# Field-pair projection on one Trainium2 core: the loop over batch tiles is replaced, on all five engines, by sixteen tiles written out

## The chip, the cores and the metric

The kernel runs on one core of one Trainium2 chip. The metric is the device time of one execution in microseconds; less is better. The core has a TensorE (PE) for matrix products, a VectorE (DVE), a ScalarE (ACT), a GpSimd (POOL), and a SyncE (SP) that here only issues transfers. Each engine has its own stream of instructions, and they meet only at semaphores. The transfers of the core are carried out by 16 DMA engines.

## The reference, cut to what matters

```python
# x: (2048, 32, 64) f32, W: (496, 64, 64) f32, PAIRS: all (i, j) with i < j < 32
xi = x[:, pi, :]
xj = x[:, pj, :]
proj = jnp.einsum('bpd,pod->bpo', xi, W)
return proj * xj                      # (2048, 496, 64) f32
```

For each of the 496 pairs of fields, field i is projected with the pair's own 64x64 matrix and multiplied element by element with field j. The input is 16.8 MB, the weights are 8.1 MB, and the output is 260 MB.

## The kernel before, in words

The batch of 2048 rows is cut into 16 tiles of 128 rows (`tiles`, line 74). All weights stay in SBUF (`w_sb`, line 134): even fields in partitions 0 to 63, odd fields in 64 to 127, so that a step works on two fields, one for each half of the rows of the PE array. A tile has 21 steps (`plan`, line 25; a step is a pair of lists of segments, one for each half), and the steps are bundled into 11 output groups. One group leaves by one DMA (line 183), whose 128 rows of 7 to 15 KB are spread over the DMA engines.

The stages of a step, each on its own engine, linked by semaphores:

- PE (`project`, line 275; matmul at line 284) writes two halves of a PSUM buffer `proj[b][h]`. The two buffers b are used in turn.
- DVE (line 326) multiplies the first half with `x_sb` and writes it to `staged`. The second half of two steps in three (`pool_steps`, line 93) is copied out by ACT (line 250) and then multiplied in place by POOL (line 213); of the other steps DVE does both halves.
- SP (lines 170 to 184) waits until a group is complete and issues its store.

`staged` has nine slots for the eleven groups of a tile: groups 9 and 10 share slots 4 and 5 with the groups of those numbers (`SHARED_SLOTS`, line 17). Before a slot is written again its last store must have landed (`slot_free`, line 156; waited for by DVE and ACT). Between steps 9 and 10 PE transposes the next tile's `x` ("turn", line 291), ACT copies it into `x_t` (line 228), and before step 3 ACT issues the load of the x tile after that (`load_x`, line 231).

Every engine's stream is an `emit(tile)` that yields one tile's instructions, and `each_tile` (line 119) strings the tiles together: tile 0 written out, then a counted loop of seven rounds over two tiles (tiles 1 to 14), then tile 15 written out. Inside the loop a tile's number is a register expression, so that the values that semaphores are waited for (`use + 1`, `tile.number + 1`, `tile.number * 16 * ...`) and the DRAM addresses of the stores and x loads (lines 183 and 237) are computed by small register instructions before the instruction that uses them. The first and the last tile have constants there. The loop is each engine's own: there is no barrier between the engines at its end.

Of the kernel before, what the change touches and what calls it, by code (L numbers as in the profile page):

```python
# [71 lines left out]
def field_pair_project(nc, x, w, ident, out, fields, dim):  # L72
    batch = x.shape[0]
    tiles = batch // P
# [40 lines left out]
    def w_needed(segments):  # L115
        to = max(w_at[i] + (j - i - 1 + n) * dim for i, j, n in segments)
        return next(c for c in range(len(w_cuts) - 1) if w_cuts[c + 1] >= to)

    def each_tile(eng, emit):
        emit(Tile(0, 0, 0))  # L120
        with eng.Fori(0, (tiles - 2) // 2) as t:  # L121
            emit(Tile(2 * t + 1, 1, t))
            emit(Tile(2 * t + 2, 0, t + 1))
        emit(Tile(tiles - 1, 1, tiles // 2 - 1, last=True))

    with ExitStack() as ctx:  # L126
# [41 lines left out]
        @block.sync  # L168
        def _(sp):
            def emit(tile):  # L170
                where = {item: (b, use) for item, b, use in items(tile)}
                for g, group in enumerate(groups):
                    first, n = group_range(g)


                    pooled = any(s in pool_steps for s in group)
                    if pooled and g == 0:
                        sp.wait_ge(pool_scaled[g], tile.number + 1)
                    b, use = where[group[-1]]
                    sp.wait_ge(emptied[b][group[-1] not in pool_steps], use + 1)  # L180
                    if pooled and g > 0:
                        sp.wait_ge(pool_scaled[g], tile.number + 1)  # L182
                    sp.dma_start(out[bass.ds(tile.number * P, P), first * dim:(first + n) * dim],  # L183
                                 staged[slot_of[g]][:, 0:n * dim]).then_inc(stored[slot_of[g]], 16)

            half = fields * dim // 2
            sp.dma_start(x_sb[0][:, 0:half], x[0:P, 0:half]).then_inc(x_first_loaded[0], 16)
            sp.dma_start(w_sb[:, w_cuts[0]:w_cuts[1]], w[:, w_cuts[0]:w_cuts[1]]).then_inc(w_loaded[0], 16)
            sp.dma_start(x_sb[0][:, half:], x[0:P, half:]).then_inc(x_first_loaded[1], 16)
            for c in range(1, len(w_cuts) - 2):  # L190
                sp.dma_start(w_sb[:, w_cuts[c]:w_cuts[c + 1]], w[:, w_cuts[c]:w_cuts[c + 1]]
                             ).then_inc(w_loaded[c], 16)

            c = len(w_cuts) - 2
            sp.dma_start(w_sb[0:dim, w_cuts[c]:w_cuts[c + 1]], w[0:dim, w_cuts[c]:w_cuts[c + 1]]
                         ).then_inc(w_loaded[c], 16)
            sp.dma_start(x_sb[1][:], x[P:2 * P, :]).then_inc(x_loaded[1], 16)

            each_tile(sp, emit)
            for k in range(slots):  # L200
                sp.wait_ge(stored[k], 16 * slot_uses[k] * tiles)

        @block.gpsimd
        def _(pool):
            def emit(tile):
                for item, b, use in items(tile):
                    if item not in pool_steps:
                        continue
                    for i, j, n in steps[item][1]:
                        product = staged_part(item, i, j, n)  # L210

                        pool.wait_ge(emptied[b][1], use + 1)  # L212
                        last = nc.gpsimd.tensor_tensor(  # L213
                            product, product, x_sb[tile.parity][:, j * dim:(j + n) * dim], ALU.mult)
                    g = group_of[item]
                    if item == max(s for s in groups[g] if s in pool_steps):
                        last.then_inc(pool_scaled[g], 1)

            each_tile(pool, emit)

        @block.scalar
        def _(act):
            act.dma_start(ident_sb[:], ident).then_inc(ident_loaded, 16)

            def turned_out(b, use, to):
                for h in range(2):
                    act.wait_ge(filled[b][h], use + 1)
                    nc.scalar.activation(x_t[to][:, h * (UNIT // P):(h + 1) * (UNIT // P), :].rearrange(  # L228
                        "p k b -> p (k b)"), proj[b][h][:], ACT.Copy).then_inc(emptied[b][h], 1)

            def load_x(tile):

                _, b, use = list(items(Tile(tile.number - 1, 1 - tile.parity, None)))[-1]

                act.wait_ge(emptied[b][1], use + 1)
                act.wait_ge(pool_scaled[group_of[pool_steps[-1]]], tile.number)
                act.dma_start(x_sb[1 - tile.parity][:], x[bass.ds((tile.number + 1) * P, P), :]
                              ).then_inc(x_loaded[1 - tile.parity], 16)

            def emit(tile):  # L240
                for item, b, use in items(tile):
                    if item == LOAD_BEFORE and not tile.first and not tile.last:
                        load_x(tile)
                    if item == "turn":
                        turned_out(b, use, 1 - tile.parity)
                    elif item in pool_steps:
                        (i, j, n), = steps[item][1]
                        slot_free(act, tile, group_of[item])
                        act.wait_ge(filled[b][1], use + 1)  # L249
                        nc.scalar.activation(staged_part(item, i, j, n), proj[b][1][:, 0:n * dim],  # L250
                                             ACT.Copy).then_inc(emptied[b][1], 1)

            turned_out(0, 0, 0)
            each_tile(act, emit)

        @block.tensor
        def _(pe):
            def turn(b, of, h):

                for n in range(UNIT // P):  # L260
                    k = h * (UNIT // P) + n
                    last = nc.tensor.transpose(proj[b][h][:, n * P:(n + 1) * P],  # L262
                                               x_sb[of][:, k * P:(k + 1) * P], ident_sb[:])
                last.then_inc(filled[b][h], 1)

            def pieces(segments):

                for (i, j, n), at in zip(segments, place(segments, dim)):
                    col, left = w_at[i] + (j - i - 1) * dim, n * dim
                    while left:  # L270
                        width = min(left, BANK - at % BANK)
                        yield i, col, at, width
                        at, col, left = at + width, col + width, left - width

            def project(tile, s, b, use):
                if tile.first:
                    for h in range(2):
                        pe.wait_ge(w_loaded[w_needed(steps[s][h])], 16)
                for h in range(2):
                    if not (tile.first and use == 0):  # L280
                        pe.wait_ge(emptied[b][h], use)
                    half = slice(h * dim, (h + 1) * dim)
                    for i, col, at, width in pieces(steps[s][h]):
                        last = nc.tensor.matmul(  # L284
                            proj[b][h][:, at:at + width], x_t[tile.parity][half, i // 2, :],
                            w_sb[half, col:col + width], start=True, stop=True)
                    last.then_inc(filled[b][h], 1)

            def emit(tile):
                for item, b, use in items(tile):  # L290
                    if item == "turn":
                        pe.wait_ge(x_loaded[1 - tile.parity], 16 * tile.half + 16)
                        for h in range(2):
                            pe.wait_ge(emptied[b][h], use)
                            turn(b, 1 - tile.parity, h)
                    else:
                        project(tile, item, b, use)

            pe.wait_ge(ident_loaded, 16)
            for _ in range(WARM_UP):  # L300
                nc.tensor.transpose(proj[1][0][:, 0:P], ident_sb[:], ident_sb[:])  # L301
            for h in range(2):
                pe.wait_ge(x_first_loaded[h], 16)
                turn(0, 0, h)
            for h in range(2):

                pe.wait_ge(emptied[0][h], 1)
            each_tile(pe, emit)

        @block.vector  # L310
        def _(dve):
# [16 lines left out]
                                x_sb[tile.parity][:, j * dim:(j + n) * dim], ALU.mult)  # L328
                        last.then_inc(emptied[b][h], 1)

            each_tile(dve, emit)


# [28 lines left out]
```

## Time and profile before

| | |
|---|---|
| time, median of 3 runs | 691.28 us (691.06 to 692.1) |
| profiled execution, its own time | 692.27 us |
| its span (first to last instruction) | 690.5 us |
| granted TensorE clock, mean | 0.904 |
| PE / PEld / DVE / ACT / POOL busy | 87 / 54 / 60 / 30 / 57% |
| moved by DMA | 285.15 MB, mean 413 GB/s |
| DMA queues: output and first loads (q1), x loads (q10) | 93.3% and 5.8% of 16 engines |
| instruction packets (q8, q14) | 5 of 16 KB, 5 of 8 KB |

Busy shares are of the span. The profiled execution is 1.0 us above the median of the three runs; 1.8 us of it lie around the span. A queue's share is the time of its packets, as a share of 16 engines' span; packets that overlap can bring a sum slightly over 100%. Register, branch, semaphore and DMA-issuing instructions are not counted as busy.

### The profile page before, as it was taken

The numbers are of one execution on the slowest core, as the hardware profiler recorded it, in microseconds if no ns is written. First come the engines' busy times: TensorE is split into PE (matmuls) and PEld (weight loads), VectorE is DVE, ScalarE is ACT, GpSimd is POOL, SyncE is SP. The second block draws the span as 40 slices with busy tenths as digits, with TensorE's granted clock in tenths as the row PEclk, the third lists the DMA queues.
The fourth block names the chain that finished last, engine by engine and source line by source line (L and its number), as shares of the span: only waits on it lengthen the run. The fifth ranks groups of instructions, "written<-read, shape, count | busy, mean of one in ns | idle before, by whom it ended". The sixth has DMA issues, their size and how long they took to land.

```text
span 690.5 us, 8403 instructions
## 1 busy us (share of the span) xinstructions
PE 597.8 (87%) x2704; PEld 372.9 (54%) x2704; DVE 415.0 (60%) x528; ACT 205.4 (30%) x257; POOL 390.7 (57%) x228
## 2 busy tenths in 40 slices
PE   6889979799797989979799797988979799797972
PEld 4556646466464555646466464645646466464641
DVE  0656646576574756647576474856747576474851
ACT  2322414233241332414223241322414224141320
POOL 0745738457474655738557374755738557374651
PEclk9998989899897998989989898997989989898995
DMA  8999999999999999999999999999999999999897
GB/s 332 386 430 425 431 427 429 426 428 427 423 427 429 392 417 411 427 426 407 428 407 431 406 427 428 412 425 376 424 423 405 428 415 423 414 423 427 357 422 316
DMA packets 29754, 285.15 MB, mean 413 GB/s; under 512 B 3312, under 2 KB 3440, under 8 KB 7216
## 3 DMA queue, kind: packets, MB, share of 16 engines
q1 hardware_dynamic: 27584, 270.28, 93.3%
q10 hardware_dynamic: 2160, 14.75, 5.8%
q8 instruction: 5, 0.08, 0.0%
q14 instruction: 5, 0.04, 0.0%
HBM read 24.97 MB, written 260.05 MB: 413 GB/s over the span
## 4 chain that ended last, share of the span: by engine, by line
DMA 37%; POOL 26%; issue 22%; PE 10%; ACT 2%; DVE 1%; POOLq 0%; SPq 0%; DVEq 0%; ACTq 0%
DMA out_dram<-staged 36%; POOL staged L213 26%; PE proj L284 9%; ACT staged L250 2%; DVE staged L326 1%; DMA ident_sb<-ident_dram 1%; PE proj L301 1%; POOLq L212 0%; PE proj L262 0%; ACT x_t L228 0%; SPq L183 0%; POOLq L121 0%; ACTq L249 0%; DVEq L126 0%; SPq L182 0%
## 5 line engine op out<-in xcount | busy, mean ns | idle before, releaser
L284 PE MATMUL proj<-w_sb,x_t 64*128 64x512 f32 (+7 forms) x2432 | 562.3, 564 | 72.5 <-DVE staged L326 70.1
L326 DVE TENSOR_TENSOR staged<-proj,x_sb 128x1024 f32<-128x1024 f32 (+7 forms) x528 | 415.0, 828 | 264.5 <-PE proj L284 187.0
L213 POOL TENSOR_TENSOR staged<-staged,x_sb 128x1024 f32<-128x1024 f32 (+4 forms) x224 | 390.5, 1755 | 284.6 <-ACT staged L250 283.8
L284 PEld LDWEIGHTS proj<-w_sb,x_t 64*128 64x128 f32 x2432 | 339.2, 205 | 288.5 <-issue 132.1
L250 ACT ACTIVATE staged<-proj 128x1024 f32<-128x1024 f32 (+4 forms) x224 | 172.8, 787 | 453.0 <-PE proj L284 344.6
L262 PEld LDWEIGHTS proj<-ident_sb,x_sb 128*128 128x128 f32 x256 | 30.4, 150 | 10.2 <-issue 7.6
L262 PE MATMUL proj<-ident_sb,x_sb 128*128 128x128 f32 x256 | 34.1, 290 | 1.9 <-DMA x_sb<-x_dram 1.9
L228 ACT ACTIVATE x_t<-proj 128x1024 f32<-128x1024 f32 x32 | 31.2, 1022 | 13.7 <-PE proj L262 12.2
L301 PE MATMUL proj<-ident_sb 128*128 128x128 f32 x16 | 3.7, 425 | 5.7 <-DMA ident_sb<-ident_dram 5.7
L301 PEld LDWEIGHTS proj<-ident_sb 128*128 128x128 f32 x16 | 3.3, 227 | 5.7 <-DMA ident_sb<-ident_dram 5.7
L228 ACT ACT_TABLE_LOAD x1 | 1.3, 1283 | 1.2 <-PEq L356 1.2
L356 POOL MEMSET const-float32-0.0<- 128x1 f32 x1 | 0.1, 98 | 0.2 <-issue 0.2
L356 POOL MEMSET const-bfloat16-1.0<- 128x1 bf16 x1 | 0.1, 101 | 0.0
L356 POOL MEMSET const-uint8-127<- 128x1 uint8 x1 | 0.1, 101 | 0.0
L356 POOL MEMSET const-float32-1.0<- 128x1 f32 x1 | 0.1, 98 | 0.0
## 6 DMA issues: line engine op xcount, KB each, us to landing
out_dram<-staged SPq DMA_DIRECT2D x16, 1952.0 KB, 11.4
out_dram<-staged SPq DMA_DIRECT2D x16, 1824.0 KB, 14.2
out_dram<-staged SPq DMA_DIRECT2D x16, 1728.0 KB, 17.3
out_dram<-staged SPq DMA_DIRECT2D x16, 1696.0 KB, 14.8
out_dram<-staged SPq DMA_DIRECT2D x16, 1568.0 KB, 14.3
out_dram<-staged SPq DMA_DIRECT2D x16, 1440.0 KB, 15.7
out_dram<-staged SPq DMA_DIRECT2D x16, 1312.0 KB, 15.6
out_dram<-staged SPq DMA_DIRECT2D x16, 1216.0 KB, 13.8
```

The source lines that it names most:

```text
L213: last = nc.gpsimd.tensor_tensor(product, product, x_sb[tile.parity][:, j * dim:(j + n) * dim], ALU.mult)
L228: nc.scalar.activation(x_t[to][:, h * (UNIT // P):(h + 1) * (UNIT // P), :].rearrange("p k b -> p (k b)"), proj[b][h][:], ACT.Copy).then_i ...
L250: nc.scalar.activation(staged_part(item, i, j, n), proj[b][1][:, 0:n * dim], ACT.Copy).then_inc(emptied[b][1], 1)
L262: last = nc.tensor.transpose(proj[b][h][:, n * P:(n + 1) * P], x_sb[of][:, k * P:(k + 1) * P], ident_sb[:])
L284: last = nc.tensor.matmul(proj[b][h][:, at:at + width], x_t[tile.parity][half, i // 2, :], w_sb[half, col:col + width], start=True, stop=True)
L301: nc.tensor.transpose(proj[1][0][:, 0:P], ident_sb[:], ident_sb[:])
L326: last = nc.vector.tensor_tensor(staged_part(item, i, j, n), proj[b][h][:, at:at + n * dim], x_sb[tile.parity][:, j * dim:(j + n) * dim], ...
L356: nc = bacc.Bacc("TRN2", target_bir_lowering=False, num_devices=1)
```

## The change

A second helper, `every_tile`, calls `emit` sixteen times with plain numbers: parity and half as before, `last` for tile 15. All five engines use it in place of `each_tile`. The tiles, their order, the steps, the waits and the transfers stay what they are; in tiles 1 to 14 the counts that are waited for and the DRAM addresses become constants, the register instructions and the seven backward branches of each engine are gone, and each engine's instruction stream is about four times as long (16 tiles of code in place of 4).

```diff
+    def every_tile(emit):
+
+        for t in range(tiles):
+            emit(Tile(t, t % 2, t // 2, last=t == tiles - 1))
+
...
-            each_tile(sp, emit)
+            every_tile(emit)
...
-            each_tile(pool, emit)
+            every_tile(emit)
...
             turned_out(0, 0, 0)
-            each_tile(act, emit)
+            every_tile(emit)
...
-            each_tile(pe, emit)
+            every_tile(emit)
...
-            each_tile(dve, emit)
+            every_tile(emit)
```

## Rows read from the trace of the kernel before

**Rows 1.** The page: instructions per engine, queues by kind (packets, MB, share)

```profile
PE 597.8 (87%) x2704; PEld 372.9 (54%) x2704; DVE 415.0 (60%) x528; ACT 205.4 (30%) x257; POOL 390.7 (57%) x228
...
q1 hardware_dynamic: 27584, 270.28, 93.3%
q10 hardware_dynamic: 2160, 14.75, 5.8%
q8 instruction: 5, 0.08, 0.0%
q14 instruction: 5, 0.04, 0.0%
```

**Rows 2.** Waits: engine line <- what: us, times, longest

```profile
ACT staged L250 <- DMA out_dram<-staged: 107.9, 16, 7.3
DVE staged L326 <- DMA out_dram<-staged: 73.7, 16, 5.2
PE proj L284 <- DVE staged L326: 70.1, 16, 5.0
...
PE proj L284 <- issue: 1.2, 1, 1.2
```

**Rows 3.** Stretches: PE, PEld, DVE, ACT, POOL busy; PEclk, DMA share, GB/s

```profile
135.00:640.00 505.00, 450.02 (x2037) 279.56 (x2039) 314.66 (x403) 154.13 (x194) 295.70 (x170) 0.91 1.00 419
...
475.00:485.00 10.00, 10.00 (x47) 5.95 (x45) 8.08 (x8) 3.78 (x4) 6.60 (x4) 0.97 0.82 333
645.10:647.30 2.20, 2.20 (x9) 1.15 (x8) 2.20 (x3) 0.81 (x1) 2.20 (x2) 1.00 0.05 22
686.40:689.20 2.80, 0.00 (x0) 0.00 (x0) 0.00 (x0) 0.00 (x0) 0.00 (x0) 0.50 0.07 30
```

**Rows 4.** The chain that ended last: two pieces of one tile (start, us)

```profile
384.08 0.71 ACT staged L250
...
409.44 16.02 DMA out_dram<-staged
```

**Rows 5.** Instruction packets in 0:135, in 135:640 (all its queues), in 640:690.5

```profile
q8 instruction: 4, 0.07, 0.2%
q14 instruction: 4, 0.03, 0.1%
...
q1 hardware_dynamic: 19410, 198.79, 93.4%
q10 hardware_dynamic: 1728, 12.58, 6.8%
...
q8 instruction: 1, 0.02, 0.2%
q14 instruction: 1, 0.01, 0.0%
```

**Rows 6.** One q8 packet in 29:31, 86:88, 647:649; one q14 packet in 76:77

```profile
q8 instruction: 1, 0.02, 3.4%
q8 instruction: 1, 0.02, 2.8%
q8 instruction: 1, 0.02, 4.1%
...
q14 instruction: 1, 0.01, 1.9%
```

**Rows 7.** DMA in 647.38:647.46: packets by queue

```profile
q8 instruction: 1, 0.02, 101.4%
q1 hardware_dynamic: 1, 0.01, 29.4%
```

**Rows 8.** Line 121, the loop's end: ns min/median/max

```profile
L121 PEldq FUSED_REGOPS  x7: 59/59/59, 53.0 to 551.5; - x7
...
L121 PEldq ALU_OP  x7: 32/32/32, 136.0 to 634.2; - x7
L121 PEldq COMPARE_BRANCH  x7: 76/208/228, 136.1 to 634.3; - x7
```

**Rows 9.** Register work of PE (L281), POOL (L212) and SP (L183) in the loop

```profile
L281 PEldq ALU_OP  x154: 32/32/42, 54.8 to 628.4; - x154
...
L212 POOLq ALU_OP  x140: 32/32/43, 61.3 to 626.3; - x140
...
L183 SPq MOVE out_dram<-staged x154: 29/29/38, 65.9 to 640.7; - x154
```

**Rows 10.** Waits of DVE (L323), of SP (L182); stores issued; time to landing

```profile
L323 DVEq EVENT_SEMAPHORE  x151: 21/21/50, 15.3 to 677.0; - x151
...
L182 SPq EVENT_SEMAPHORE  x144: 17/17/17, 22.9 to 675.6; - x144
...
L183 SPq DMA_DIRECT2D out_dram<-staged x176: 332/332/427, 20.9 to 679.6; - x176
...
DMA to landing us min/median/max: 9.4/14.6/18.6
```

## Prediction, made before the change was built

> **What bounds the kernel now.** I read the page first, then the DMA share by stretches, then the waits, then the instruction packets. The page [rows 1] puts PE at 87% and no other engine over 60%, but the two data queues together at 93.3 + 5.8 = 99.1% of 16 DMA engines. That says: transfers. The reader should not stop at this mean. The waits [rows 2] say the same from the other side: once per tile (16 times) ACT waits 107.9 / 16 = 6.7 us, DVE 73.7 / 16 = 4.6 us for a store to land and give its slot of `staged` back, and PE waits 70.1 / 16 = 4.4 us behind DVE. So each tile of about 41 us (two of them per round of the loop, (634.3 - 136.1) / 6 = 83 us [rows 8]) holds a pause of 4.4 us or more on every compute engine, and that is their spare time. The chain of waits [rows 4] shows the same leg once per tile, a store of 16.0 us from issue to landing, while 2 MB at 419 GB/s [rows 3] would take 5 us: a store stands some 10 us in the queue behind others. Line 183's median to landing is 14.6 us [rows 10].
>
> The stretches say more [rows 3]. From 135 to 640 us the share is 1.00. But from 645.1 to 647.3 it is 0.05, and at the end, 686.4 to 689.2, it is 0.07. One engine of 16 is 0.06. So in these stretches one DMA engine still works off its part of the stores, while the other 15 have finished theirs and have nothing more. In 475 to 485 the share is 0.82: the 15 pause there too, for about 1.8 us. A store's slot is free only when all 16 parts have landed, so the compute engines wait for the laggard, and the laggard alone has work without a break. My reading: one DMA engine is a little slower than the rest, it is busy from the first transfer to 689 us, and the time of the kernel is the sum of its packets. Whatever does not touch that engine's work costs or saves nothing, up to the spare time above.
>
> Here the Trainium skill speaks, in "DMA: Bandwidth & Descriptors", section "Latency and other measured facts": engines 7 and 15 are usually slower in traces, but it ties that to transfers that GpSimd sets up, and says that the kind used here (q1 and q10 are hardware queues) has not that cause. The trace shows a laggard on the hardware queue all the same; which number it has is not shown. By the page's cause there would be no lasting laggard, and every added packet would cost only a sixteenth of its length, 0.1 us each.
>
> **What the change removes.**
> - Seven backward branches on each engine. On PE one costs 59 + 32 + 208 = 0.30 us at the median [rows 8], so 2.1 us in the whole kernel.
> - Register arithmetic before waits and transfers. PE has 154 such operations of 32 ns on the line that waits for empty buffers (4.9 us in all, 0.35 us per tile), POOL 140 of 32 ns (4.5 us, 0.32 us per tile), SP 154 moves of 29 ns (4.5 us) before its stores [rows 9]. DVE and ACT have similar ones.
>
> None of this is on the laggard DMA engine. What covers it is the pause at the slot: an engine that comes 0.5 us earlier through a tile waits 0.5 us longer for the same landing. SP issues a store some tenths of a microsecond earlier, and the store stands 10 us in the queue either way. Value taken: 0. If the cover were gone, it would be worth up to 0.35 us (PE's arithmetic) + 0.15 us (half a branch) = 0.5 us per tile, 7 us over tiles 1 to 14; both ends are kept, as a rival.
>
> The change adds no wait and moves no transfer past another. In tiles 0 and 15 nothing changes.
>
> **What it adds: instruction packets.** PE's code comes in packets of 0.08 MB / 5 = 16 KB [rows 1]. Four of the five fall in the first 135 us, none from 135 to 640 us, and one after 640 us [rows 5]. So while tiles 0 to 2 run for the first time, code is loaded at one packet per 30 us; the loop's second and later rounds load nothing, and the code of the last tile is loaded after the loop. Written out, PE's code is new all the time: one packet per 30 us from 30 us to about 673 us is (673 - 30) / 30 = 21 to 22 packets in place of 5, so 16 to 17 more. The other engines have instructions in 8 KB packets (0.04 / 5). Their work and waits add up to 528 + 257 + 228 instructions [rows 1] + 151 + 144 waits + 176 stores [rows 10] = about 1,500, against 5,408 for PE: by PE's density (5,408 in about 22 packets of 16 KB) that is 12 packets of 8 KB, so about 7 more than the 5 seen.
>
> In bytes this is 0.33 MB on top of 285, or 0.8 us at 419 GB/s if 16 equal engines shared it. But one packet lies on one DMA engine. Its own time is its share times 16 engines times the window: 0.034 x 16 x 2 = 1.1 us at 29 us, 0.028 x 32 = 0.9 us at 87 us, 0.041 x 32 = 1.3 us at 647 us; an 8 KB packet is 0.019 x 16 = 0.3 us [rows 6]. I take 1.2 us and 0.4 us, as something is lost in going from queue to queue.
>
> Which engine gets them decides the price. Of one packet the trace tells: at 647.38 us the instruction packet begins, and within 80 ns of it, with the 15 others still out of work, an output packet begins too [rows 7]. The output packet is the laggard's, so the instruction packet went to another engine. The fetches have their own queue and may be spread over all engines. Bounds: none of the 16 to 17 on the laggard, 0 us; all of them, 17 x 1.2 = 20 us. I take the even spread, as no engine could have been loading each time without being seen behind the laggard: 17 / 16 = about one packet on the laggard, 1.2 us, and 7 / 16 of an 8 KB one, 0.2 us. Packets on the other 15 are hidden by their lead of several microseconds.
>
> **Sum.** For the profiled execution: 692.27 + 0 + 1.2 + 0.2 = 693.7 us. Against the median of the runs, 1.0 us lower, the same step gives 691.28 + 1.4 = 692.7 us.
>
> **The other rule of the skill that bears on this.** PE's branches cost 0.21 us each and no instruction packet accompanies them [rows 5, 8]: the loop's body of two tiles, three packets long, stays on the engine. "Runtime: NRT & Kernel Launch", section "Instruction fetch mechanics", says that a taken branch to code outside a window of two pages has to fetch it first, which is one reason why kernels prefer to be fully written out. By it each of seven rounds would stall PE for a packet of 1.3 us, 9 us in all, and the change would give that back as far as it is not covered. The trace does not agree: no fetch in 505 us. The page also says that straight code is prefetched and mostly hidden.
>
> **The rivals.**
> - *Instruction packets miss the laggard, or are so few that nothing shows.* Time 691.3 us, within 0.3 of before. For it: the one packet that can be placed missed it. Against: some 24 new packets and 16 engines. Chance 0.18.
> - *Slower by much: the fetches have one home.* If PE's packets all go to one engine, that engine gets 17 x 1.2 = 20 us more. If it is the laggard, 711 us. If it is another, it decides as soon as its extra exceeds its lead; of the lead 1.8 + 2.1 + 2.6 = 6.5 us are visible as pauses [rows 3], so at most 20 - 6.5 = 13.5 us more, 705 us. For it: each packet is on one engine whole. Against: [rows 7] rules out the laggard for at least one. Chance 0.07 (0.02 of it the laggard).
> - *Slower by PE waiting for code.* PE goes through a packet in 30 us; when one comes late, PE stands. It decides from 4.4 us per tile on, as less is covered [rows 2]. With 1.4 packets per tile it would take over 3.1 us of standing for each; as long as a store stands in the queue (some 10 us), 14 - 4.4 = 10 us per tile. Against: four packets came in the first 135 us beside a full queue, and all that PE's matmuls waited for nothing but their own issue is 1.2 us, once [rows 2]. A few late ones would cost 2 to 4 us, 694 to 695 us. Chance 0.06.
> - *Faster: the compute path sets the pace after all* and the pauses of the 15 engines are its mark. Then 0.5 us per tile comes back: 691.3 - 7 = 684 us at most, 688 us if half. For it: the chain of waits runs through compute between its DMA legs, and 15 engines do run dry. Against: the laggard never does, and slots wait for it. Chance 0.07.
> - *The change does not do what it says,* for instance the branches stay. Time 691.3 us; the diff leaves no room for it, so under 0.01, counted with the first.
>
> **How the numbers follow.** My forecast has 0.62: 692.7 us, with its own range from 691.8 (one small packet, a light one) to 694.5 us (two PE packets and one of the others on the laggard, 2.4 + 0.4 us). With the missed laggard (690.8 to 691.8) and the mild form of late code (to 695.5) the range 690.8 to 695.5 us holds about 0.85; what is left out is the single home of the packets, the strong late code and the compute path. 0.2% is 1.4 us, about what a measurement can tell from no change, so "slower" begins at 692.7 us, in the middle of my forecast. Slower: half of 0.62 plus 0.07 + 0.06 = 0.44, and same: 0.31 + 0.18 = 0.49, faster 0.07.
>
> **What the profile of the changed kernel would show.** Right: about 22 packets of 16 KB on q8, one per 30 us to the end; no register operations at lines 212, 281 and 323; the waits of ACT and DVE for stores longer by about 0.5 us per tile; an end where again the share is 0.06 for some 3 us. Wrong: an end in which all 16 stop together (no laggard), pauses of PE put down to issue at every 30 us, a longer lone engine at the end and in mid-kernel, or waits for stores that shrink by as much as the time does.

## The result

| | before | with the change |
|---|---|---|
| median of 22 runs each | 691.31 us (691.05 to 692.49) | 690.35 us (689.87 to 691.32) |
| ratio to before, 95% interval | | 0.9986 (0.998 to 0.9992) |
| profiled execution, its span | 690.5 us | 688.3 us |

The change makes the kernel faster by 0.14%, some 1.0 us, with an interval that excludes no change and stays at or inside 0.2%. I had forecast 1.4 us in the other direction, with 690.8 us as the lower end of the range. The sign was wrong, and the time lies outside.

The page of the changed kernel: the span and the number of instructions, then the engines, then the DMA queues.

```profile
span 688.3 us, 7400 instructions
...
PE 597.6 (87%) x2704; PEld 371.0 (54%) x2704; DVE 414.4 (60%) x528; ACT 205.2 (30%) x257; POOL 390.7 (57%) x228
...
q1 hardware_dynamic: 27584, 270.28, 93.6%
q10 hardware_dynamic: 2160, 14.75, 5.6%
q8 instruction: 21, 0.34, 0.2%
q14 instruction: 16, 0.13, 0.1%
```

Against [rows 1] the work is the same to the instruction, and the output and x traffic is the same to the packet. Two things differ. The instruction packets went from 5 to 21 on q8, as the prediction had counted (21 to 22), and from 5 to 16 on q14, where it had counted about 12. And the page of the kernel before begins with another number of instructions:

```profile
span 690.5 us, 8403 instructions
```

So 1,003 fewer are executed. Its waits and stretches (columns as in [rows 2] and [rows 3]):

```profile
ACT staged L256 <- DMA out_dram<-staged: 103.8, 16, 7.8
DVE staged L332 <- DMA out_dram<-staged: 71.3, 16, 5.7
PE proj L290 <- DVE staged L332: 67.7, 16, 5.5
...
PE proj L290 <- issue: 1.2, 1, 1.2
...
135.00:640.00 505.00, 454.48 (x2048) 281.86 (x2048) 314.61 (x405) 154.02 (x193) 294.81 (x171) 0.91 1.01 421
475.00:485.00 10.00, 10.00 (x50) 5.95 (x46) 8.59 (x9) 3.26 (x5) 8.54 (x4) 1.00 0.94 374
684.20:687.00 2.80, 0.00 (x0) 0.00 (x0) 0.00 (x0) 0.00 (x0) 0.00 (x0) 0.50 0.08 35
```

And the instruction packets of its stretch from 135 to 640 us, in which the loop had none [rows 5]:

```profile
q8 instruction: 16, 0.26, 0.2%
q14 instruction: 12, 0.10, 0.1%
```

There is still an engine alone at the end (share 0.08), so the laggard exists. But the pauses for stores did not grow by 0.5 us per tile, as they must where compute gets quicker and the transfers do not. They shrank: ACT's from 107.9 to 103.8 us, PE's from 70.1 to 67.7 us [rows 2]. That is the sign named in the prediction as speaking against it, waits that shrink by as much as the time. And the DMA engines together moved 421 GB/s in place of 419 [rows 3]. So it looks as if the transfers themselves had become quicker, in spite of 27 packets more. Each of these is one profiled execution against one, and e4 below, at an unchanged time, has pauses that differ from before by 1.5 us, so this is a hint and not yet a proof.

### The profile page after: what moved, and what is told of

It reads as the page before. It is cut to its first block, busy times and chain, and to the rows that moved or that the text cites. A ratio compares the mean times of both kernels' runs of the same rounds, so it can differ in the third digit from the quotient of the medians.

```text
span 688.3 us, 7400 instructions
## 1 busy us (share of the span) xinstructions
PE 597.6 (87%) x2704; PEld 371.0 (54%) x2704; DVE 414.4 (60%) x528; ACT 205.2 (30%) x257; POOL 390.7 (57%) x228
## 3 DMA queue, kind: packets, MB, share of 16 engines
q10 hardware_dynamic: 2160, 14.75, 5.6%
## 4 chain that ended last, share of the span: by engine, by line
PE 48%; DMA 37%; POOL 5%; ACT 4%; DVE 3%; issue 1%; ACTq 0%; DVEq 0%; SPq 0%
PE proj L290 48%; DMA out_dram<-staged 36%; POOL staged L219 5%; ACT staged L256 4%; DVE staged L332 3%; DMA ident_sb<-ident_dram 1%; PE proj L307 1%; ACT x_t L234 0%; PE proj L268 0%; ACTq L255 0%; DVEq L132 0%; SPq L188 0%; DVEq L329 0%
## 5 line engine op out<-in xcount | busy, mean ns | idle before, releaser
L290 PE MATMUL proj<-w_sb,x_t 64*128 64x512 f32 (+7 forms) x2432 | 564.7, 565 | 70.0 <-DVE staged L332 67.7
L268 PEld LDWEIGHTS proj<-ident_sb,x_sb 128*128 128x128 f32 x256 | 27.9, 141 | 10.6 <-issue 7.6
L268 PE MATMUL proj<-ident_sb,x_sb 128*128 128x128 f32 x256 | 31.5, 276 | 2.4 <-DMA x_sb<-x_dram 2.4
```

What stands on the lines that cost most here:

```text
L290: last = nc.tensor.matmul(proj[b][h][:, at:at + width], x_t[tile.parity][half, i // 2, :], w_sb[half, col:col + width], start=True, stop=True)
```

## The experiments

Theory A, formed on this result: the kernel's time is set by one lagging DMA engine, as predicted; but that engine is not slow by itself. Each instruction that any compute engine executes slows it by a few nanoseconds. The change takes away 1,003 instructions (a gain) and adds instruction packets (the predicted cost). "Executed" means here what the page counts in its first line: register, branch and waiting instructions too. Theory B: the register work and the branches lay on a compute path that sets the time. C: only SP's instructions matter, as SP issues the stores. D: the laggard is slow by itself, with no cause outside.

**One part of the change alone.** In e1 only `pe` calls `every_tile`, in e2 all but `pe`:

```diff
-            each_tile(pe, emit)
+            every_tile(emit)
```

> Only PE is written out; the other four keep the loop. Theory A (the lagging DMA engine sets the time, and each instruction that any engine executes slows it by 2 to 3 ns, apart from the instruction packets it is given): 196 instructions fewer give -0.5 us, one of PE's 16 more packets falls on the laggard and gives +1.2 us, so +0.7 us against before, between 0 and +1.5. Theory B (register work and branches lie on a compute path that sets the pace): PE's 0.5 us per tile come back, -3 to -7 us if all of the path is PE, -0.4 us if PE has its share by instructions of the measured 1.0 us.

Measured: 0.9997 of before (0.9988 to 1.0006), with 8,206 instructions and 21 and 6 instruction packets.

> SP, ACT, POOL and DVE are written out, PE keeps the loop. Theory A: about 800 instructions fewer give -2.0 us, some 11 more packets of 8 KB cost up to +0.3 us on the laggard, so -1.7 us against before: more than the whole change gave (-1.0), since PE's packets are not there. Theory B: the share of the four engines, -0.6 us, and never more than the whole change.

Measured: 0.9991 (0.9983 to 1.0), that is -0.6 us, with 7,597 instructions. The two parts do not speak for theory A: its -1.7 us for e2 lies outside the interval (-1.2 to 0 us), B's -0.6 us in it. But each effect is about a microsecond or less, and so is the interval. What they do tell: neither part is a loss of a microsecond, and none gives 3 us.

**More instructions, no more work.** e3 adds to the kernel before:

```diff
                                  staged[slot_of[g]][:, 0:n * dim]).then_inc(stored[slot_of[g]], 16)
+                    with sp.Fori(0, 4):
+                        sp.wait_ge(ident_loaded, 16)
```

> The kernel before with a loop of four rounds on SP behind each of the 176 store issues, each round a wait that is met at once: about 2,400 more instructions, no longer code for the other engines, no bytes, nothing on the compute path (SP is idle for microseconds there). Theory A: +5 to +7 us, laggard with more left to do alone at the end. Theory B and the forecast's own reading (only packets burden the laggard): 0, within 0.5 us.

Measured: 1.0061 (1.0048 to 1.0074), +4.2 us. Its page begins with

```profile
span 693.7 us, 9987 instructions
```

The wait is carried by another instruction of the round, so 1,584 more are executed and not 2,400: 4.2 / 1,584 = 2.7 ns each (2.1 to 3.2 by the interval). The line of the added loop, in SP's stream, shows what they are:

```profile
L185 SPq ALU_OP  x704: 32/33/52, 20.3 to 684.0; - x176
L185 SPq COMPARE_BRANCH  x704: 40/45/54, 20.4 to 684.0; - x176
```

e5 adds them elsewhere, on POOL, behind each of its steps:

```diff
+                    for _ in range(6):
+                        pool.wait_ge(ident_loaded, 16)
```

> The kernel before with six waits that are met at once behind each of POOL's 14 steps per tile: 84 x 16 = 1,344 more instructions, all of one kind, on another engine than in e3, 17 ns each where POOL is idle anyway. Theory A (each executed instruction costs the lagging DMA engine a fixed time, e3 measured 4.4 us / 1,584 = 2.8 ns): +3.7 us. Theory C (e3's cost comes from SP alone, the engine that issues the stores): 0, within 0.5 us.

Measured: 1.0025 (1.0015 to 1.0035), +1.7 us:

```profile
span 690.8 us, 9076 instructions
```

Waits go two to an instruction, so it is 673 more and not 1,344. That is 2.6 ns each (1.5 to 3.6), in agreement with e3, from another engine and another kind of instruction. Theory C falls. That POOL itself had become the path is unlikely: in e4, which comes next, POOL is busy for 13 us more (404.1 in place of 390.7) and the time does not change.

**The path made longer.** e4 adds one multiplication per tile on DVE:

```diff
+                    if item in (DELAY_AT,):
+                        nc.vector.tensor_tensor(scratch[:], x_sb[tile.parity][:, 0:896],
+                                                x_sb[tile.parity][:, 0:896], ALU.mult)
```

> The kernel before with one more multiplication per tile on DVE, 128x896 in SBUF into a scratch buffer, 0.9 us, behind the slot wait and ahead of step 19: 16 more instructions in all. Theory A and the forecast: within 0.5 us of before, DVE's and ACT's wait for stores about 0.9 us per tile shorter. Theory B: 0.9 us per tile on the path, up to +14 us.

Measured: 1.0005 (0.9996 to 1.0013). The operation took 2.4 us, not 0.9, at the same number of instructions:

```profile
L323 DVE TENSOR_TENSOR scratch<-x_sb x16: 2440/2442/2452, 52.5 to 671.8; 128x896 f32<-128x896 f32 x16
```

39 us of work cost nothing that can be measured. But the pauses did not shrink either (ACT's wait for stores was 109.4 us, PE's behind DVE 71.5), so the operation had fallen into DVE's own idle time, and as a test of the path it is weak. e14 lengthens PE's stream, by doing the first eight transposes of each turn twice:

```diff
-                for n in range(UNIT // P):
+                for n in list(range(UNIT // P)) * (2 - h):
```

> The kernel before with the first eight transposes of each turn done twice: 8 more matmuls and weight loads per tile, some 2.3 us of PE's time, ahead of all that waits for PE, and 256 instructions in all. e4's extra work fell into DVE's own idle time and did not lengthen the path; this one does, as PE has no idle time but the pause. Theory A: the pause of 4.4 us per tile covers it, 256 instructions cost +0.6 us, so 691.5 to 692.5 us, and PE's wait behind DVE shrinks from 70 to about 35 us. Theory B: 2.3 us x 15 tiles, +35 us.

Measured: 1.0007 (0.9998 to 1.0016), +0.5 us. PE is busy for 611.0 us, 13 us more than before (the second writing of a transpose was cheaper than I put it), and its wait went down by 12 us:

```profile
PE 611.0 (89%) x2832; PEld 385.0 (56%) x2832; DVE 415.0 (60%) x528; ACT 205.2 (30%) x257; POOL 390.9 (57%) x228
...
PE proj L284 <- DVE staged L326: 58.2, 16, 4.8
```

The pause covers the work one to one, as predicted, and what is left is the size of the price of 256 instructions (0.6 us), though no change at all is inside the interval too. PE's path does not set the time; theory B falls on this side.

**Fewer instructions.** e12 leaves out, in tiles 2 to 15, the products of the second PSUM bank of each half; the stores stay the same:

```diff
                     for i, col, at, width in pieces(steps[s][h]):
+                        if tile.number >= 2 and at >= BANK:
+                            continue
```

> The changed kernel without the products of the second PSUM bank of each half in tiles 2 to 15 (that is left out: DVE, ACT and POOL work on what the bank held before, so the stores and their sizes are the same). Some 14 x 76 matmuls and as many weight loads are not executed, about 2,100 instructions, and PE's written-out code is shorter by some 8 packets. Theory A: 2.8 us per 1,000 instructions, -6 us, and -0.5 us for the packets, so 683 to 685 us. Theories B, C, D and the forecast's own reading (laggard slow by itself, PE off the path): 689.8 to 690.4 us.

Measured: 0.9927 of before (0.9914 to 0.9941), and so 0.9927 / 0.9986 = 0.994 of the changed kernel, -4.1 us.

```profile
span 685.2 us, 5608 instructions
...
PE 503.9 (74%) x1808; PEld 237.9 (35%) x1808; DVE 406.8 (59%) x528; ACT 206.9 (30%) x257; POOL 389.9 (57%) x228
...
PE proj L292 <- DVE staged L334: 135.5, 26, 9.7
```

PE does 94 us less, and its wait behind DVE grows from 67.7 to 135.5 us (26 times in place of 16). Had PE been on the path, tens of microseconds were there to be won. What came is 4.1 us for 1,792 instructions and seven packets of 16 KB fewer, 2.3 ns per instruction if all is put on these. I had expected 6 us, for 2,100 instructions at 2.8 ns. This run takes away the matmuls' reading and writing of SBUF and PSUM together with the instructions, so by itself it cannot tell the two apart; e3 and e5, whose instructions touch no data, can.

e6 and e13 take away only waits for a slot that the same engine has already asked for in this tile, e6 in the changed kernel and e13 in the kernel before:

```diff
+            if g in asked:
+                return
+            asked.add(g)
```

> The changed kernel, in which DVE and ACT wait for a slot only at the first step of each group in a tile and not again at the others: about 13 waits fewer per tile, some 200 in all. Theory A: -0.6 us against the changed kernel, that is 689.8 us, -1.5 us against before. Theory B or C: as the changed kernel, 690.3 us.

> The kernel before, loop and all, in which DVE and ACT wait for a slot only at the first step of each group in a tile: about 200 waits fewer and about as many register instructions that served them, with no instruction packet more. Theory A: -400 x 2.8 ns = -1.1 us against before, about 690.2 us, the same as writing everything out. Others: 691.3 us. e6 did the first half of this on the changed kernel and showed no gain; this tells whether waits count less than other instructions.

Measured: e6 0.9986 of before (0.9977 to 0.9995), the same as the changed kernel, with 7,188 instructions (212 fewer); e13 1.0 (0.9991 to 1.0009), with 8,289 (114 fewer, not 400). By 2.3 to 2.7 ns these would be -0.5 and -0.3 us, inside both intervals. They neither help nor hurt theory A.

**The code without the saving.** e10 puts waits that are met at once back into the changed kernel, on PE, POOL, ACT, DVE and SP, in tiles 1 to 14. The edit on SP, for one:

```diff
+                    if not (tile.first or tile.last):
+                        for _ in range(6):
+                            sp.wait_ge(ident_loaded, 16)
```

> The changed kernel, with about as many waits that are met at once put back (on the same engines, tiles 1 to 14) as the change removed register instructions: the written-out code and its instruction packets stay, the number of executed instructions is that of before. Theory A: what is left against before is the price of the packets, by my forecast +1.4 us (692.7 us); if the packets are cheaper than I put them, 691.3 to 692 us. Theory B (the time of the register work on the compute path): also about before. Theory E (constants in place of registers help by themselves, not by number): as the changed kernel, 690.3 us.

Measured: 1.0046 (1.0032 to 1.006), +3.2 us against before.

```profile
span 694.3 us, 8576 instructions
...
q8 instruction: 22, 0.36, 0.2%
q14 instruction: 22, 0.18, 0.1%
```

This is the run that answers where the gain came from. The code is written out and has constants throughout, as in the changed kernel; the number of instructions is again that of before, and 173 more. The whole gain is gone, and with it 3.2 us more. So constants do not help by themselves. What the packets cost it tells less well. Against before, 173 instructions at 2.5 ns are 0.4 us, and the other 2.8 us would be the price of 34 packets. But against the changed kernel e10 has only 1,176 instructions and seven packets more, six of them of 8 KB, and is 1.0046 / 0.9986, or 4.1 us, slower. At 2.5 ns the instructions are 2.9 us of that, and some 1.2 us are left for seven packets. Either these cost more than their number would suggest, or the added waits cost more than 2.5 ns (3.5 ns would cover all); no run separates the two.

**Only the stores.** e8 leaves out all products and the later loads of x. SP issues the 176 stores, each behind the last store of its slot.

> What is left out: all products, and the later loads of x. DVE clears the nine slots once, then SP issues the same 176 stores, each behind the store before it of its slot; all else is idle, so about 400 instructions are executed in all. Theory A: no DMA engine lags; all 16 end within 0.5 us of each other, at a full rate of 425 to 430 GB/s, so 260 MB in 610 us and some 20 us ahead of them: about 630 us. If the lagging engine is slow by itself (theory D), it ends some 20 us after the others and the time is about 650 us.

e9 adds, on POOL:

```diff
+            with pool.Fori(0, 1000):
+                for _ in range(8):
+                    pool.wait_ge(filled_once, slots)
```

> As e8 (products and later loads of x left out), with POOL going through 1,000 rounds of eight waits that are met at once: about 10,000 more instructions that touch no data. Theory A: one DMA engine falls behind by 2.8 ns per instruction, up to 28 us, and the time grows by as much as the others cannot take over: +20 to +28 us against e8. Theories C and D: 0 against e8.

Measured: e8 647.37 us, e9 652.95 us, in two runs each that agree to 0.1 us. First e8, then e9; stretches (only DVE and POOL are listed there, then PEclk, DMA share, GB/s) and the page's first line:

```profile
span 645.5 us, 239 instructions
...
600.00:635.00 35.00, 0.00 (x0) 0.00 (x0) 1.00 1.01 424
644.80:645.40 0.60, 0.00 (x0) 0.00 (x0) 1.00 0.00 0
```

```profile
span 651.1 us, 6239 instructions
...
600.00:635.00 35.00, 0.00 (x0) 0.00 (x0) 1.00 1.01 424
645.50:650.50 5.00, 0.00 (x0) 0.00 (x0) 1.00 0.05 23
```

In e8 no engine lags: the share goes from full to 0 by 644.8 us (in the kept trace the 16 last output packets end between 644.1 and 644.5 us). In e9, with the same transfers and 6,000 instructions on POOL that touch no data, one engine is alone from 645.5 to 650.5 us, at a share of 0.05. That is the pattern of [rows 3], made on purpose. The time grows by 5.6 us. So no DMA engine is slow by itself with these stores, and theory D falls. This does not show that all of the full kernel's lag comes from instructions. (I had put e8 at 630 us. The slots were cleared until 29 us, and the rate was 424 GB/s.) The price is 5.6 / 6,000 = 0.9 ns per instruction, though, against 2.3 to 2.7 ns in the full kernel, and theory A as I had put it, with 2.8 ns, would have asked for 17 us. The kept traces show where the time lies: the packets of output and loads are 27,360 in both runs, and their times, added up, are 10,267.6 us in e8 and 10,273.8 in e9. The 6.2 us more are about the lag, so as far as a sum can tell some packets last longer, and no pauses come in between them. e15 has three engines (POOL, ACT and PE) each go through 2,000 rounds, in place of e9's loop:

```diff
+            with pe.Fori(0, 2000):
+                pe.wait_ge(filled_once, slots)
```

> As e8 (products and later loads of x left out), with POOL, ACT and PE each going through 2,000 rounds of a wait that is met at once: about 12,000 more instructions, from three engines at once, over in some 250 us. e9 gave +5.6 us for 6,000 instructions of one engine, 0.9 ns each, less than half of the 2.2 to 2.8 ns in the full kernel. If the price is per instruction, whichever engine executes it and however densely: +11 us. If it is 2.3 ns for short instructions of any engine: +28 us. If only a free rate matters (dense instructions are cheaper because they are handled together): under +5 us.

Measured: 766.66 us, but that is PE's own loop, which lasts to 764.5 us, long after the last store; that time tells nothing. The stores can be read apart. In e15's stretches one engine is alone again, and the DMA's rate from 640 to 670 us, in 40 slices, shows that the other 15 end near 652 us and it near 663 us. Before them stands the branch of PE's loop:

```profile
L221 PEldq COMPARE_BRANCH  x2000: 76/208/221, 29.8 to 764.5; - x182
...
655.00:658.00 3.00, 0.00 (x0) 0.00 (x0) 1.00 0.06 26
...
GB/s 473 393 410 420 547 344 512 360 382 417 416 466 380 408 416 311 23 23 37 18 37 18 37 13 26 26 39 19 29 29 0 0 0 0 0 0 0 0 0 0
```

The row has 40 slices of 0.75 us: full to the 16th (652 us), one engine's 13 to 39 GB/s to the 30th (662.5 to 663 us). Against e8's end before 644.8 us the last store is 18 us later, for up to 12,000 instructions: 1.5 ns each. The price is not the same in every setting. The packets' times add up to 10,290.7 us here, 23 us more than in e8.

**The laggard relieved.** e11 is the changed kernel with each later load of x in two pieces:

```diff
+                for r, n in ((0, 120), (120, 8)):
+                    act.dma_start(x_sb[1 - tile.parity][r:r + n, :],
+                                  x[bass.ds((tile.number + 1) * P + r, n), :]
+                                  ).then_inc(x_loaded[1 - tile.parity], 16)
```

> The changed kernel with each later load of x cut into rows 0 to 119 and rows 120 to 127. If a transfer of 120 rows is spread over 15 DMA engines and the one left out is the lagging one, that one has 5% of its bytes less (0.9 of 17.8 MB), up to 34 us of its work; the others then set the time, whose pauses and lead are some 8 to 14 us: 677 to 683 us. If the lagging engine is among those that get more, +2 to +5 us: 693 to 695 us. If a transfer of 120 rows is not spread so, no change, 690.3 us.

Measured: 1.0163 of before (1.0147 to 1.0179), +12 us against the changed kernel. It was a miss, outside every outcome that was named. The packets of q10 rose from 2,160 to 2,258, by 7 for each of 14 loads, which fits a closing packet from 15 engines and from 8 in place of one from each of 16. So some engines get nine rows where they had eight, 0.3 us in each load, and at most 5 us of the 12 can be accounted for in this way. Where the rest comes from is open, and which engine lags too.

**All in one table.** The full kernels, with instructions executed, packets on q8 and q14, and time against before, each against executions of before taken beside it (e11 is left out, as its transfers differ):

| kernel | instructions | q8, q14 | ratio |
|---|---|---|---|
| before | 8,403 | 5, 5 | 1 |
| changed | 7,400 | 21, 16 | 0.9986 |
| e1 | 8,206 | 21, 6 | 0.9997 |
| e2 | 7,597 | 5, 16 | 0.9991 |
| e3 | 9,987 | 5, 6 | 1.0061 |
| e4 | 8,403 | 5, 5 | 1.0005 |
| e5 | 9,076 | 5, 6 | 1.0025 |
| e6 | 7,188 | 21, 13 | 0.9986 |
| e10 | 8,576 | 22, 22 | 1.0046 |
| e12 | 5,608 | 14, 16 | 0.9927 |
| e13 | 8,289 | 5, 4 | 1.0 |
| e14 | 8,659 | 6, 5 | 1.0007 |

A least-squares fit of ratio x 691.3 us to a constant, the instructions, and the packets (one of 8 KB counted as a third, by their durations [rows 6]) gives 2.3 ns per instruction and 0.07 us per 16 KB packet. For the change that makes -1,003 x 2.3 ns = -2.3 us and (16 + 11 / 3) x 0.07 = +1.4 us, together -0.9 us; measured were -1.0 us. The change is itself one of the twelve kernels fitted, so this is no independent proof.

The price per instruction is the firmer of the two for these kernels: it is 2.1 to 2.4 ns also without e10, and with the two kinds of packet counted apart. The price per packet is not. The largest misses are e1 (1.2 us), e10 (0.9 us) and e2 (0.7 us), the runs with one kind of packet alone among them. Without e10 it falls to 0.04 us, with an uncertainty of 0.02. Fitted apart, the 8 KB packets cost 0.13 us each and the 16 KB ones 0.02, which is their uncertainty; the misses are then half as large, 0.5 us at most. So what the written-out code costs seems to go with the four other engines' code, and not with PE's large packets, on which the prediction had put 1.2 of its 1.4 us. That is read from a table, not from a run that was made for it.

## Why the prediction was wrong, point by point

- *What bounds the kernel: one lagging DMA engine, with the compute engines' pauses as spare time.* Right, as far as PE goes: e14 (13 us more on PE, 12 us less pause) and e12 (94 us less on PE, 4 us gained) show it from both sides. For the other engines there is only e4, which is weak.
- *The laggard is "a little slower than the rest", and "whatever does not touch that engine's work costs or saves nothing".* This sentence is the step that failed. I had taken the laggard for a property of the chip and asked only what bytes the change gives it. e8 and e9 show that an engine lags when instructions are executed elsewhere (5.6 us for 6,000), and e3 and e5 that such instructions cost the full kernel time, 4.2 and 1.7 us, with no byte more for the laggard. One clue was there: the page "DMA: Bandwidth & Descriptors" of the Trainium skill, section "Latency and other measured facts", gives no reason for a laggard on this kind of queue. I noted the contradiction and kept the laggard as a given.
- *What the change removes: value 0.* The working (no effect through the compute path) holds, but the term was mis-sized: some 1,000 executed instructions fewer were worth 2.3 us, by the fit, and 2.7 us at the price of e3.
- *What the change adds: 16 to 17 packets on q8 and about 7 on q14, 1.4 us.* 16 and 11 were seen, one q8 packet per 31 to 32 us to the end (16 in 505 us). The fit puts them at 1.4 us, the forecast's own number, but that is in part luck. e1, with 16 of the large packets more and few instructions less, was 0.2 us faster than before where the fit asks for 0.7 us more. Nothing shows a large packet falling on the laggard for 1.2 us, and the term is not secure to better than about a microsecond.
- *The rivals.* The compute path would have given 684 to 688 us; the sign was that of this rival, and by e14 and e12 the mechanism was not, on PE's side. Of late code there is no sign: PE's matmuls waited 1.2 us for their own issue, as before [rows 2]. One home for all packets would have cost 14 to 20 us, which e1 excludes.
- *The signs named beforehand.* The packets, the register lines and the lone engine at the end came as described. The waits for stores shrank where they should have grown, and that was the sign named against.
- *The Trainium skill's rule that kernels prefer to be written out* ("Runtime: NRT & Kernel Launch", section "Instruction fetch mechanics"). The direction came true by 1.0 us, but for another reason than the fetching at branches that it names. The kernel before fetched nothing at its branches [rows 5], and with the instructions put back the written-out code was 3.2 us slower than the loop (e10).

What is not settled: by which way an executed instruction loads a DMA engine. The trace holds one record for every instruction executed, and the records have to be written somewhere. The Trainium skill, "NOTIFIC — the notification-queue block", sections "The implicit engine gate" and "The coalescer", says that a fully traced engine emits records for every instruction, each a write of 16 bytes, and that four can be gathered into one write. This would fit a price per instruction of whatever kind, on whatever engine. It does not by itself explain the sizes: the price was 0.9 ns in e9 (6,000 instructions in some 555 us), 1.5 ns in e15, where they came at more than twice that rate at first, and 2.3 to 2.7 ns in the full kernel, with its 12 instructions per us. No run here switched the records off, so it is an explanation that was argued and not shown. If it holds, the lag that instructions cause belongs to the measurement: every execution timed here has a span and a granted clock on record, and without the recording the written-out kernel might gain nothing or lose. Nor is it shown why one engine of 16 bears it.

## What to carry to other kernels

Where the DMA engines set the time, look for stretches in which their share is a sixteenth: they show that one engine sets it, and it is worth asking what else loads that one. Here the number of instructions executed did, at 1 to 3 ns each on SP, on POOL, and on three engines together, so in a transfer-bound kernel that is timed as these were, the instruction count in the page's first line belongs into the sum, even where every instruction is hidden. Writing a loop out trades register instructions for instruction packets; here that came to -2.3 and about +1.4 us, the second with much doubt, and the sign depends on which of the two weighs more.

## What the runs showed of the hardware that I had not expected

- One DMA engine falls behind the 15 others in step with instructions executed on the compute engines: none behind with 239 instructions (e8), alone for over 5 us at the end with 6,239 (e9), and some 11 us with up to 12,241 (e15).
- Instructions that touch no data and are not on the path cost 2.7 ns (SP, e3) and 2.6 ns (POOL, e5) of the kernel's time.
- PE kept a loop of two tiles, three packets of 16 KB, for 505 us without another fetch [rows 5]; written out it took 16 packets in the same stretch, and its matmuls waited for their own issue no longer than in the loop (1.2 us in all).
- A DVE multiplication of 128x896 with all operands in SBUF took 2.44 us beside POOL's work on SBUF (e4), where the kernel's larger ones of 128x1024, with one operand in PSUM, took 1.22 us in the mean. POOL's multiplications of 128x512 went up too, from 1.27 to 1.44 us in the mean.
